# Index columns of both edge loops by small SyncE transfers, and the second loop's one-hot made by ScalarE

## The reference, cut to what matters

```python
row, col = edge_index                              # source and destination of each edge
# layer 0: spline convolution
basis = _basis(edge_attr_2)                        # 9 numbers per edge
messages = einsum('ek,ei,kio->eo', basis, x[row], weight)
out = zeros.at[col].add(messages) / max(degree, 1) + x @ root_w.T + root_b
x = layernorm(x + out)
# layer 1: tensor product with a radial net
R = relu(edge_weight[:, None] @ w1 + b1) @ w2 + b2 # 384 numbers per edge
Y = spherical_harmonics(edge_attr_3)
msg = products of R, Y and x[src], 32 per edge
x = layernorm(x + zeros.at[dst].add(msg))
```

## Time and profile before

| | us |
|---|---|
| median of 3 runs (lowest, highest) | 8945.88 (8944.8, 8947.13) |
| the profiled execution, its own time | 8946.99 |
| its span, first to last instruction | 8945.2 |
| PE busy | 7724.0 (86%) |
| POOL busy | 6287.4 (70%) |
| DVE busy | 5922.9 (66%) |
| ACT busy | 974.6 (11%) |

### The profile page before, as it was taken

The page is one execution under the profiler, slowest core; times in us unless marked ns, Lnnn a source line. Parts: engine busy times, 40 slices in busy tenths (PEclk is TensorE's granted clock), DMA queues, the critical chain, the costliest instruction groups (busy, mean ns, idle before and its releaser), DMA issues. The chain is left out here.

```text
span 8945.2 us, 132828 instructions
## 1 busy us (share of the span) xinstructions
PE 7724.0 (86%) x41451; PEld 5367.3 (60%) x41451; DVE 5922.9 (66%) x14667; ACT 974.6 (11%) x3157; POOL 6287.4 (70%) x6757
## 2 busy tenths in 40 slices
PE   4888888888888888888389999999999999999997
PEld 4777777777777777777244444444444444444444
DVE  5333333333333333333599999999999999999997
ACT  0000000000000000000011111111111111111110
POOL 3777777777777777775077777777777777777774
PEclk6555555555555555555599999999999999999998
DMA  1000000000000000000122222222222222222221
GB/s 44 13 13 13 13 13 13 13 13 13 13 13 13 13 13 13 13 13 10 45 57 57 59 59 60 59 58 60 58 60 58 59 59 57 59 59 60 59 57 38
DMA packets 222143, 327.63 MB, mean 37 GB/s; under 512 B 105054, under 2 KB 155119, under 8 KB 221247
## 3 DMA queue, kind: packets, MB, share of 16 engines
q0 software_dynamic: 200000, 205.20, 12.1%
q1 hardware_dynamic: 22122, 122.16, 4.9%
HBM read 320.54 MB, written 6.40 MB: 37 GB/s over the span
## 5 line engine op out<-in xcount | busy, mean ns | idle before, releaser
L432 PE MATMUL sums_ps<-hot,spread 128*96 128x64 f32 (+1 forms) x18750 | 3118.6, 369 | 404.3 <-DVE spread L373 404.3
L432 PEld LDWEIGHTS sums_ps<-hot,spread 128*96 128x96 f32 (+1 forms) x18750 | 3049.1, 281 | 577.0 <-issue 447.9
L373 DVE TENSOR_TENSOR spread<-own_ps,rows 128x1440 f32<-128x1440 f32 x625 | 1035.9, 1657 | 2403.5 <-DMA rows<-in_x,idx_a 1300.6
L291 POOL DMA_INDIRECT rows<-table_dram,idx_a x1875 | 1882.3, 1004 | 631.8 <-issue 533.2
L291 POOL DMA_INDIRECT rows<-in_x,idx_a x1875 | 1774.7, 946 | 636.4 <-issue 523.3
L291 POOL DMA_INDIRECT rows<-table_dram,idx_b x1250 | 1334.1, 1067 | 441.5 <-issue 342.8
L787 PE MATMUL radial_x<-edge_t,hidden 128*128 128x384 f32 x3750 | 1381.8, 504 | 205.1 <-DVE edge_t L910 117.7
L291 POOL DMA_INDIRECT rows<-in_x,idx_b x1250 | 1183.3, 947 | 443.9 <-issue 337.8
L799 PE MATMUL sums_ps<-edge_t,hot 128*64 128x272 f32 x11000 | 1398.6, 397 | 2.7 <-DVE edge_t L926 2.7
L787 PE MATMUL radial_y<-edge_t,hidden 128*128 128x384 f32 x2500 | 975.0, 512 | 236.6 <-DVE edge_t L910 236.5
L799 PEld LDWEIGHTS sums_ps<-edge_t,hot 128*64 128x64 f32 x11000 | 767.7, 136 | 653.0 <-DVE acc L942 146.7
(11 more groups left out here) (133 smaller groups left out, 4406.6 us busy)
## 6 DMA issues: line engine op xcount, KB each, us to landing
dist_ab<-in_edge_weight SPq DMA_DIRECT2D x125, 480.0 KB
dist_ab<-in_edge_weight SPq DMA_DIRECT2D x125, 320.0 KB
rows<-in_x,idx_a POOLq DMA_INDIRECT x1875, 2.4
rows<-table_dram,idx_a POOLq DMA_INDIRECT x1875
rows<-in_x,idx_b POOLq DMA_INDIRECT x1250, 2.4
rows<-table_dram,idx_b POOLq DMA_INDIRECT x1250, 2.5
acc<-in_edge_attr SPq DMA_DIRECT2D x1, 4687.5 KB
table_dram<-edge_t SPq DMA_DIRECT2D x1, 4687.5 KB
```

The lines of the kernel that those rows point to most:

```text
L291: pool.indirect_dma_start(out=rows[u if own else SLOT[u]][:, j, 0:width], out_offset=None, in_=table, in_offset=bass.IndirectOffsetOnAxis( ...
L373: dve.tensor_tensor(spread[s][:, :, 0:K].rearrange("e t (k c) -> e t k c", c=C), basis[s].unsqueeze(3).to_broadcast([P, G, 9, C]), rows[s] ...
L432: last = pe.matmul(sums_ps[s][0:m, c * WINDOW:(c + 1) * WINDOW], spread[s][:, j, c * CH:c * CH + m], hot[s][:, j, :], start=(j == 0 and c ...
```

## The change

- A new helper `load_indices` issues a transfer from `src_t` to an index tile: half 0 is 15 columns of 128 partitions (7.5 KB), half 1 is 10 columns (5 KB). SP issues both, in both loops, once per block each. POOL's copies are gone; POOL waits for the landings instead, and in loop two its gathers of units 0 and 3 wait for the slot's last user five units back like the others.
- In both loops SP loads half 1 of a block once the whole block before has been used (spread_ready, or prods_ready[1]), then waits until the rows of units 0, 1 and 2 of the block have landed, and loads half 0 of the next block. In loop two this stands behind the two distance loads in SP's program.
- In loop two DVE no longer makes `hot`. ACT makes it behind `hidden`, in two steps: five activations Abs(rel - window), one per tile, and after a wait on its own semaphore one Relu(1 - that) over all five, in place. Before them it waits until the slot's last user has been summed. With whole numbers that is the same one-hot.
- A tile `one` (a column of 1.0), and semaphores for these steps.

```diff
--- before.py
+++ after.py
@@ -268,35 +268,35 @@
     return values
 
 
-def pool_gathers(nc, pool, keep, table, idx, rows, width, idx_ready, gathers_begun, rows_used, rows_landed):
+def load_indices(sp, keep, idx, idx_landed, half, i):
+
+    first, n = ((0, 3 * G), (3 * G, 2 * G))[half]
+    sp.dma_start(idx[half][:, :], keep["src_t"][:, bass.ds(i * (U * G) + first, n)]).then_inc(idx_landed[half], 16)
+
+
+def pool_gathers(nc, pool, keep, table, idx, rows, width, idx_landed, gathers_begun, rows_used, rows_landed):
 
     own = len(rows) == U
-
-    src_t = keep["src_t"]
     passes = load_passes(pool, keep)
 
-    def gather(g, i, u):
-
-        ago = {0: 3, 3: 4}.get(u, U) if own else AGO[u]
-        pool.wait_ge(rows_used, g * U + (u - ago + 1 + CREDIT))
+    def gather(g, u):
+
+        pool.wait_ge(rows_used, g * U + (u - (U if own else AGO[u]) + 1 + CREDIT))
         if u in (0, 3):
-
-            n = 3 if u == 0 else 2
-            pool.tensor_copy(idx[u // 3][:, 0:n * G], src_t[:, bass.ds(i * (U * G) + u * G, n * G)]).then_inc(idx_ready, 1)
-            pool.wait_ge(idx_ready, g * 2 + (1 + u // 3))
-
+            pool.wait_ge(idx_landed[u // 3], (g + 1) * 16)
         pool.sem_inc(gathers_begun, 1)
         for j in range(G):
             column = (u % 3) * G + j
-            pool.indirect_dma_start(out=rows[u if own else SLOT[u]][:, j, 0:width], out_offset=None, in_=table,
+            slot = u if own else SLOT[u]
+            pool.indirect_dma_start(out=rows[slot][:, j, 0:width], out_offset=None, in_=table,
                                     in_offset=bass.IndirectOffsetOnAxis(ap=idx[u // 3][:, column:column + 1], axis=0)
-                                    ).then_inc(rows_landed[u if own else SLOT[u]], 16)
+                                    ).then_inc(rows_landed[slot], 16)
 
     with pool.Fori(0, passes) as p:
         with pool.Fori(0, B) as i:
             g = p * B + i
             for u in range(U):
-                gather(g, i, u)
+                gather(g, u)
 
 
 def spline_edges(nc, keep, x, weight0):
@@ -327,8 +327,9 @@
         window_ps = own_ps[:, 0:WINDOW]
         basis = [own_ps[:, WINDOW + n * 9 * G:WINDOW + (n + 1) * 9 * G].rearrange("e (t k) -> e t k", k=9) for n in range(SLOTS)]
         gathers_begun, window_ready = sem("l0_gathers_begun"), sem("l0_window_ready")
-        step, wk_landed, wk_ready, idx_ready = sem("l0_step"), sem("wk_landed"), sem("wk_ready"), sem("l0_idx_ready")
+        step, wk_landed, wk_ready = sem("l0_step"), sem("wk_landed"), sem("wk_ready")
         rows_landed = [sem(f"l0_rows_landed{n}") for n in range(SLOTS)]
+        idx_landed, indices_done = [sem("l0_idx_a_landed"), sem("l0_idx_b_landed")], sem("l0_indices_done")
         basis_ready, spread_ready, hot_ready = sem("basis_ready"), sem("spread_ready"), sem("l0_hot_ready")
         summed, sums_ready, msg_ready, added = sem("summed"), sem("sums_ready"), sem("l0_msg_ready"), sem("l0_added")
         block = ctx.enter_context(nc.Block())
@@ -338,10 +339,27 @@
             sp.wait_ge(wk_ready, 1)
             for c in range(3):
                 sp.dma_start(wk[0:CH, c, 0:C], weight0[3 * c:3 * c + 3].rearrange("k i o -> (k i) o")).then_inc(wk_landed, 16)
+            passes = load_passes(sp, keep)
+            load_indices(sp, keep, idx, idx_landed, 0, 0)
+            with sp.Fori(0, passes) as p:
+
+                def body(i, after):
+                    g = p * B + i
+                    sp.wait_ge(spread_ready, g * U + CREDIT)
+                    load_indices(sp, keep, idx, idx_landed, 1, i)
+                    for u in range(3):
+                        sp.wait_ge(rows_landed[SLOT[u]], filled(g, u, 16 * G))
+                    load_indices(sp, keep, idx, idx_landed, 0, after)
+
+                with sp.Fori(0, B - 1) as i:
+                    body(i, i + 1)
+                body(B - 1, 0)
+            sp.wait_ge(idx_landed[0], passes * (B * 16) + 16)
+            sp.sem_inc(indices_done, 1)
 
         @block.gpsimd
         def _(pool):
-            pool_gathers(nc, pool, keep, x, idx, rows, C, idx_ready, gathers_begun, spread_ready, rows_landed)
+            pool_gathers(nc, pool, keep, x, idx, rows, C, idx_landed, gathers_begun, spread_ready, rows_landed)
 
         @block.vector
         def _(dve):
@@ -693,6 +711,7 @@
         hidden = ring("hidden", [P, G * P])
         hot = ring("hot1", [P, G, WINDOW])
         rho5 = ring("rho5", [P, G, 5])
+        one = sbuf("one", [P, 1])
         red = ring("red", [P, 2 * 16])
         along = sbuf("along", [P, G, MUL])
 
@@ -712,10 +731,12 @@
         sums_ps = [psum(f"sums1_ps{n}", [P, 512]) for n in range(SLOTS)]
         TURN = 320
         gathers_begun = sem("l1_gathers_begun")
-        step, idx_ready, w_landed, w_zero, w_ready = sem("l1_step"), sem("l1_idx_ready"), sem("w_landed"), sem("w_zero"), sem("w_ready")
+        step, w_landed, w_zero, w_ready = sem("l1_step"), sem("w_landed"), sem("w_zero"), sem("w_ready")
         rows_landed = [sem(f"l1_rows_landed{n}") for n in range(U)]
+        idx_landed, indices_done = [sem("l1_idx_a_landed"), sem("l1_idx_b_landed")], sem("l1_indices_done")
         dist_landed = [sem("dist_a_landed"), sem("dist_b_landed")]
         hidden_ready, hot_ready, rho_ready = sem("hidden_ready"), sem("l1_hot_ready"), sem("rho_ready")
+        window_ready, apart_ready = sem("l1_window_ready"), sem("apart_ready")
         dots_ready, turns_ready, inputs_ready = sem("dots_ready"), sem("turns_ready"), sem("inputs_ready")
         radial_ready = [sem("radial_x_ready"), sem("radial_y_ready")]
         prods_ready = [sem("prods_x_ready"), sem("prods_y_ready")]
@@ -731,20 +752,37 @@
                 sp.dma_start(w1c[HID * h:HID * (h + 1), :], w1.rearrange("o h -> h o")).then_inc(w_landed, 16)
                 sp.dma_start(b1c[HID * h:HID * (h + 1), :], b1.rearrange("(h o) -> h o", o=1)).then_inc(w_landed, 16)
             passes = load_passes(sp, keep)
+            load_indices(sp, keep, idx, idx_landed, 0, 0)
+
+            def load_dist(g, i, h):
+                u0, u1 = DIST[h]
+                sp.wait_ge(hidden_ready, g * U + (u1 - U + CREDIT))
+                part = edge_weight[bass.ds(i * (U * G * P) + u0 * G * P, (u1 - u0) * G * P)]
+                sp.dma_start(dist_ab[HID * h:HID * (h + 1), 0:(u1 - u0) * G * P],
+                             part.rearrange("(o e) -> o e", o=1).to_broadcast([HID, (u1 - u0) * G * P])
+                             ).then_inc(dist_landed[h], 16)
+
             with sp.Fori(0, passes) as p:
-                with sp.Fori(0, B) as i:
+
+                def body(i, after):
                     g = p * B + i
-                    for h, (u0, u1) in enumerate(DIST):
-
-                        sp.wait_ge(hidden_ready, g * U + (u1 - U + CREDIT))
-                        part = edge_weight[bass.ds(i * (U * G * P) + u0 * G * P, (u1 - u0) * G * P)]
-                        sp.dma_start(dist_ab[HID * h:HID * (h + 1), 0:(u1 - u0) * G * P],
-                                     part.rearrange("(o e) -> o e", o=1).to_broadcast([HID, (u1 - u0) * G * P])
-                                     ).then_inc(dist_landed[h], 16)
+                    load_dist(g, i, 0)
+                    load_dist(g, i, 1)
+                    sp.wait_ge(prods_ready[1], g * U + CREDIT)
+                    load_indices(sp, keep, idx, idx_landed, 1, i)
+                    for u in range(3):
+                        sp.wait_ge(rows_landed[u], (g + 1) * (16 * G))
+                    load_indices(sp, keep, idx, idx_landed, 0, after)
+
+                with sp.Fori(0, B - 1) as i:
+                    body(i, i + 1)
+                body(B - 1, 0)
+            sp.wait_ge(idx_landed[0], passes * (B * 16) + 16)
+            sp.sem_inc(indices_done, 1)
 
         @block.gpsimd
         def _(pool):
-            pool_gathers(nc, pool, keep, table_dram, idx, rows, ROW, idx_ready, gathers_begun, prods_ready[1], rows_landed)
+            pool_gathers(nc, pool, keep, table_dram, idx, rows, ROW, idx_landed, gathers_begun, prods_ready[1], rows_landed)
 
         @block.scalar
         def _(act):
@@ -754,6 +792,7 @@
             passes = load_passes(act, keep)
 
             with act.Fori(0, passes) as p:
+                act.wait_ge(window_ready, p + 2)
                 with act.Fori(0, B) as i:
                     g = p * B + i
                     for u in range(U):
@@ -770,6 +809,13 @@
                         act.activation(hidden[s][0:HID, :], dist[u], ACT.Relu, bias=b1c[HID * h:HID * (h + 1), 0:1],
                                        scale=w1c[HID * h:HID * (h + 1), 0:1]
                                        ).then_inc(hidden_ready, 1)
+                        act.wait_ge(summed, freed(g, u))
+                        for j in range(G):
+                            last = act.activation(hot[s][:, j, :], keep["window"][:, :], ACT.Abs,
```

(10 more changed lines are left out.)

## The result

The changed kernel takes **8509.12 us** (median of 4 runs, 8508.27 to 8509.61) against 8945.83 for the kernel before on the same chip: ratio 0.9512, 95% interval 0.9495 to 0.9528, 437 us less. The prediction was 8517, with a range of 8490 to 8620.

The account below looks back on a forecast made before the run. POOL was taken to bound loop one and VectorE loop two; 8947 less 180 us for the index copies and 250 us for the one-hot, with transfers and ScalarE at cost 0, gave 8517 us, range 8490 to 8620.

Parts of the forecast that it names:

- What bounds each loop: Before the change, POOL sets loop one's pace at 32.7 us per block, VectorE loop two's at 34.9.
- Index copies: Loop one: without POOL's two copies a block takes 31.25 us instead of 32.69, saving 180 us in all.
- One-hot: Loop two: moving it off VectorE saves 0.40 us a piece, five per block, 250 us in all.
- Index transfers at no cost: Both loops: SP's two small transfers per block, about 2 us each, stay hidden; cost 0.
- The cover of 8.4 us: Loop two: time free for half B's transfer, asked for after the last block's products, before VectorE wants unit 3's rows.
- Stalls: Loop two: POOL's gather stalls fall from 2.1 to about 1.2 us per block, as VectorE's run of two-SBUF-input instructions ends sooner.
- Rival 1: Loop two: stalls stay at 2.1 us, POOL bounds at 33.35 per block; 194 us saved instead of 250, total 8573; chance 0.14.
- TensorE's shortest unit: Loop two: TensorE needs at least 6.4 us per unit, against VectorE's 6.3 after the change.
- Rival 2: Loop two: TensorE's 6.4 per unit and VectorE's offset load add up; 212 us saved, total 8555; chance 0.07.
- ScalarE: Loop two: six more instructions, 1.9 us per unit, cost 0; busy time near 2160 us.
- Rivals 3 and 4: First: loop two, L878 hits every next gather, 8717, chance 0.05. Second: loop one, TensorE takes 31.9 per block, 8597, 0.04.
- Rival 5: Both loops: index transfers land late behind SP's distances; slower beyond 11.4 us latency, 9342 at 13 us; chance 0.05.

## Why the prediction was right

- **What bounds each loop** held: POOL in loop one, VectorE in loop two, shown by the run with the index transfers alone (nothing gained in loop two) and by the aligned offsets (everything gained).
- **Index copies**, 180 us: 187 measured between the first and the last gather. A gather's step, which I took as 1.25, is 3900.6/125/25 = 1.248 without copies, and a block took 4088.1/125 = 32.70 before, where my one reading gave 32.69.
- **One-hot**, 250 us: 258. From the start of the third product to that of the reduction it is 0.194 us now (L928 to L961, mean over loop two), where it was 0.599 with the one-hot between; 0.405 x 625 = 253. The other 5 us lie at the loop's ends.
- **Index transfers at no cost** held. The latency, 2 us, is 1.8 in the median, and 2.66 from the products to the first gather. The cover of 8.4 us in loop two was mis-sized: it is about 10, since some 1.5 us that VectorE works between its products and the next block's load were left out. The total did not depend on it.
- **Stalls**, 1.2 us (0 to 2.1): 0.6. POOL stays below VectorE's 32.9, as forecast, but the reason was half right. That a gather waits for the end of the one-hot is shown; that a shorter run of two-input instructions means a smaller sum is refuted (0.3 us per block with one such instruction more, 1.8 with a reduction in its place). So how much the sum fell was in part luck of the phase. Rival 1 kept 2.1 and did not come.
- **TensorE's shortest unit**, 6.4: too long. In the changed kernel it does most units in 6.2 to 6.3 (radial_x to radial_x). Its busy time per block fell from 32.1 to 3555/112.6 = 31.6 with the same work, so part of the busy time had been waiting. Rival 2 (8555) rested on that figure.
- **ScalarE**, 2160 us busy: 2123. The Abs are 335 ns each by the group's mean, 0.26 apart, the Relu 562. Hidden, as the ten more Abs show.
- Rivals 3 and 4 did not come: VectorE waits for rows 3 times in loop two, and loop one is at 31.2. Rival 5, the slower side, is real as a mechanism in loop two and starts at about 10 us between products and first gather, where the changed kernel has 2.7; loop one's side of it was not tested.
- What I had not in the sum: 8 us at the edges of the loops; by luck they offset half of the 16 us by which the two savings were larger.

## What to carry to other kernels

When two engines are each within a few per cent of a loop's pace, relieving one shows its worth only once the other is relieved too: 182 and 206 us alone were 437 together. Moving small index work to an idle queue costs nothing as long as the steps from its release to its use are longer than its latency, and that cover can be counted from the order of the programs before anything is built. A high busy share of a pipelined engine (92% for TensorE in loop two before) is no floor: ask what it waits for inside.

## What the runs showed of the hardware that I had not expected

- An indirect transfer's issue on GpSimd, 0.94 us, becomes up to 1.9 us long: it ends 0.82 us behind the end of a VectorE instruction with two SBUF inputs that runs 0.12 us after the issue's start (476 of 479 long gathers in one run). Beside an instruction with one SBUF input there is no such delay (13 gathers beside a reduction at 943 to 947 ns, 1653 beside products with PSUM at most 973). Where the gather comes first, the VectorE instruction is the longer one (0.33 instead of 0.27).
- Between two engines that touch like this, the phases lock: the changed kernel's blocks of loop two repeat to 0.02 us (33.02 to 33.04, each fourth 32.43 to 32.44), and one unused instruction more can halve the stalls (0.3 us per block for 0.6) or triple them (1.8).
- A sequencer's load of five words takes 0.59 us from a multiple of four words, and 1.18 from elsewhere.
- A VectorE instruction on partitions 64 to 127 between others that start at partition 0 cost 0.12 us more in front of it (0.31 where 0.19 is usual) and 0.12 behind it (0.52 where the one-hot of the same size had 0.40). Both runs with it write into the tile `acc`; that the partitions and not the tile cost it is my reading.
